# Eleven idle products of TensorE in the two gaps of a routing chain

## The chip, the cores and the metric

The kernel runs on one core of one Trainium2 chip. The metric is device time in microseconds, the median of several runs. A profiled execution gives the rows shown below; it is an execution of its own, with its own time.

## The reference

A graph layer, a linear attention and a mixture of experts on 1250 rows of 512 numbers. What matters here is the last part, the mixture:

```
x  = x + gnn(xn, ...) + mix(xn, ...)          # xn = layernorm(x)
xt = layernorm(x)
logits = xt @ Ws + bs                         # 1250 x 8
probs  = softmax(logits); prob_max = max(probs); routes = argmax(probs)
y[e]   = gelu(xt @ W1[e] + b1[e]) @ W2[e] + b2[e]
out    = x + prob_max * y[routes]
```

Each row goes through one of eight experts, the one with its largest logit.

## The kernel before

The rows stand in 10 tiles of 125 (t). The kernel is written by hand, one program for each engine, and the engines wait for each other by semaphores (`wait_ge`). TensorE takes its products in the order in which they are written. The names below are those of the code.

At the end of the graph layer TensorE turns the updated rows (`x2_turn`, line 817) and forms the logits (`route`, line 824), with products of 128 x 8. Then follows the routing chain:

- VectorE scales the logits, finds the largest of each row and writes the expert one-hot `oh16` (line 1407). ScalarE and VectorE form `prob_max`; it goes with the row's mean and deviation into `factors`, which SyncE's queue stores to `x1_rows` in DRAM (line 470).
- TensorE waits for `route_ok` 1 and multiplies the one-hot by triangles and ones (ten products of line 863, one of line 866). That counts the rows of each expert and gives each row its place.
- VectorE makes of this the row one-hot `row_hot` and `chunk_tag` (lines 1414 to 1435). The rows are put in 17 chunks of 128, each of one expert.
- TensorE waits for `route_ok` 2 and multiplies them (ten products of line 872). The result is the list of the rows of each chunk, which VectorE turns into `get_i` (line 1444) and `out_i`.
- TensorE then runs `MOE_UP` = 12 idle products (line 875): the identity by a constant of 250 columns, in float32, written to a part of bank 5 that nobody reads.
- GpSimd waits for the stores of all rows, for the store of `factors` (`fac_st`) and for `get_i` (`id_ok`), and then gathers the chunks by indirect DMA (line 507), eight of them ahead.

For each chunk c ScalarE normalizes the gathered rows (`xs_norm`, line 1745), TensorE turns them (`xs_turn`, line 883), ScalarE copies the result out of the bank (line 1752), and TensorE runs `up` (line 892, eight products with the weights of the chunk's expert), `h_turn` (line 902) and `down` (line 569, six products). The order on TensorE is xs_turn(0), up(0), xs_turn(1), and then h_turn(c), up(c+1), xs_turn(c+2), down(c). Meanwhile the rest of the second expert weight is split in a high and a low part, by ScalarE (`w2_high`, line 1702) and by VectorE (`w2_low`, line 1377, after `out_i`).

Of the kernel before, what the change touches and what calls it, by code (L numbers as in the profile page):

```python
# [34 lines left out]
WIN = 250  # L35
# [22 lines left out]
RESET_AT = 511  # L58
HALF = 112
MOE_UP = 12  # L60
LEFT = 25
RUN_UP = 10

# [48 lines left out]
def build(nc, x, edge_src, edge_dst, edge_w, consts, halves, biases, small, fold, wqkv, wp, bvt, w1f, w2f, b2f, out):  # L112
    with ExitStack() as ctx:
# [20 lines left out]
        def const(name):  # L134
            a, w = CONSTS[name]
            return cst[:, a:a + w]
# [13 lines left out]
        ident, ones = const("ident"), const("ones")  # L150
# [142 lines left out]
        bank = [banks[:, i, :] for i in range(8)]  # L293
# [232 lines left out]
        def _(pe):  # L526
# [7 lines left out]
            for i in range(NL):  # L534
                pe.wait_ge(hot_ok, next(n for n, m in enumerate(MARKED) if i < m) + 1)
                for h in range(2):
                    mm = pe.matmul(bank[1 + h][:, 0:NBH * LC], half("before")[0:TP, :],
                                   hot[:, i, h * NBH:(h + 1) * NBH, :].rearrange("p b c -> p (b c)"),
                                   start=(i == 0), stop=(i == NL - 1))
# [5 lines left out]
                      start=True, stop=True).then_inc(total_ps, 1)  # L545
# [65 lines left out]
            for k in range(2):  # L611
                mm = pe.matmul(bank[4][0:TP, 0:MD].rearrange("p (a n) -> p a n", a=2),
                               bm_col[:, k:k + 1].to_broadcast([128, TP]), w1g[:, :, k, :],
                               start=(k == 0), stop=(k == 1))
# [22 lines left out]
            for k in range(KD):  # L637
                pe.matmul(bank[5][0:TP, 256:256 + E], ones[:, 0:TP], little("ws")[:, k * E:(k + 1) * E], start=(k == 0),
                          stop=(k == KD - 1), skip_group_check=True)
# [57 lines left out]
            for n in range(PCOLS // 2):  # L697
                pe.wait_ge(sort_hot, n + 1)
                pe.wait_ge(sort_act, n + 1)
                for j in range(2):  # L700
                    for v in range(VT):
                        mm = pe.matmul(bank[1 - v // 2][:, v % 2 * NCH:(v % 2 + 1) * NCH], row_1h[:, n % RS, v, :, j],  # L702
                                       chunk_1h[:, n % RS, :, j], start=(n == 0 and j == 0 and v % 2 == 0),
                                       stop=(n == PCOLS // 2 - 1 and j == 1), skip_group_check=True)
# [126 lines left out]
            def both(step, w):  # L831
                step(2 * w)
                step(2 * w + 1)
# [23 lines left out]
            both(x2_turn, 4)  # L857
            both(route, 4)

            pe.wait_ge(route_ok, 1)  # L860
            for t in range(NT):
                n = NT - t
# [2 lines left out]
                               stop=False, skip_group_check=True)  # L865
            mm = pe.matmul(bank[7][0:TP, 0:NT * E], half("before")[0:TP, 0:TP], oh16[:, :, :].rearrange("p t e -> p (t e)"),
                           start=False, stop=True, skip_group_check=True)
            mm.then_inc(route_ps, 1)

            pe.wait_ge(route_ok, 2)  # L870
            for t in range(NT):
                mm = pe.matmul(bank[6][:, 0:NC], row_hot[:, t, :], chunk_tag[:, t, :], start=(t == 0), stop=(t == NT - 1))
            mm.then_inc(route_ps, 1)
            for _ in range(MOE_UP):
                pe.matmul(bank[5][:, 0:WIN], ident, const("cols"), start=True, stop=True)
# [56 lines left out]
        def _(dve):  # L932
# [66 lines left out]
            def pick(i):  # L999
# [7 lines left out]
                left = NB  # L1007
                while left > LEFT:
                    half_ = -(-left // 2)
# [3 lines left out]
                with nc.allow_low_precision(reason="whole numbers up to SLOTS, one of them not zero"):  # L1013
                    dve.tensor_reduce(slot_i[:, a:b], slot_p[:, 0:LEFT, 0:b - a].rearrange("p b c -> p c b"), X,
                                      ALU.max).then_inc(pick_ok, 1)
# [469 lines left out]
        def _(act):  # L1485
# [4 lines left out]
            def x_sums(a, b):  # L1490
                act.wait_ge(ld_x[next(i for i, (_, n) in enumerate(X_PARTS) if a < n)], 32)
                for t in range(a, b):
                    last = act.activation(q_sb[:, t, :], rec[:, t, 0:D], ACT.Copy, accum_out=x_sum[:, 0, t:t + 1])
                last.then_inc(sum_ok, b - a)
                act.wait_ge(sum_ok, b)
                act.activation(x_sum[:, 1, a:b], x_sum[:, 0, a:b], ACT.Copy, scale=-D ** -1.5).then_inc(mean_ok, b - a)
# [18 lines left out]
            def norm(t):  # L1515
                act.wait_ge(rstd_ok, next(g for g, (_, b) in enumerate(STATS) if t < b) + 1)
                if t >= 2:
                    act.wait_ge(xT_ps, t - 1)
                act.activation(xn[:, t % 2, :], rec[:, t, 0:D], ACT.Identity, bias=nmr[:, t:t + 1],
                               scale=rstd[:, t:t + 1]).then_inc(xn_ok, 1)  # L1520
# [339 lines left out]
```

## Time and profile before

| | |
|---|---|
| median of 3 runs | 494.15 us (493.7 to 494.18) |
| the profiled execution | 493.5 us |
| its span | 491.4 us |
| TensorE busy | 424.5 us (86%) |
| VectorE busy | 366.9 us (75%) |
| ScalarE busy | 298.3 us (61%) |
| GpSimd busy | 194.8 us (40%) |
| share of TensorE in the chain that ended last | 64% |

The span runs from the first to the last instruction of the program; the profiled execution's time has 2.1 us more. In the rows, PE is TensorE, DVE is VectorE, ACT is ScalarE, POOL is GpSimd and SP is SyncE; PEld is TensorE's weight load, and L863 is line 863 of the kernel. PEclk is the clock that TensorE was granted, as a share of full speed: 1.00 is 2.4 GHz and 0.50 is 1.2 GHz. Shares of busy time are means over stages with different limits.

### The profile page before, as it was taken

Reading aid. Unit: us, or ns where it says so; the run is one execution under the profiler, and the core shown is the slowest. Engines: PE = TensorE matmul, PEld = TensorE weight load, DVE = VectorE, ACT = ScalarE, POOL = GpSimd, SP = SyncE. Lnnn points to the kernel's source line nnn. Section 1 sums busy time; section 2 is a strip of 40 time slices with the busy share of each in tenths; the row PEclk is TensorE's granted clock in tenths of the full one; section 3 lists DMA queues with packets and bytes.
Section 4 is the critical chain, followed back from the end, with each engine's and each line's share of the span. In section 5 each row is a group of like instructions: output and inputs, shape, how many; then the busy total and the mean of one; then the engine's idle time right before and its main releaser. Section 6 shows DMA issues by size and latency. Waiting matters only on the chain.

```text
span 491.4 us, 8811 instructions
## 1 busy us (share of the span) xinstructions
PE 424.5 (86%) x2701; PEld 343.4 (70%) x2701; DVE 366.9 (75%) x717; ACT 298.3 (61%) x845; POOL 194.8 (40%) x160
## 2 busy tenths in 40 slices
PE   3665999999999999999777777899898957999992
PEld 1454887888887788877555555799876746788881
DVE  6786688877786888698999998478279874455552
ACT  4577999988897123363777777554335662666550
POOL 0378878688887787870000000000000008254321
PEclk9878999999999999999999999999999858999998
DMA  7992000000000000005000000000006964243210
GB/s 228 284 250 49 1 3 3 1 4 2 3 3 1 2 2 3 2 3 191 2 1 2 1 2 0 3 1 0 1 1 258 412 225 128 74 120 110 68 65 16
DMA packets 15742, 31.07 MB, mean 63 GB/s; under 512 B 7652, under 2 KB 8283, under 8 KB 14675
## 3 DMA queue, kind: packets, MB, share of 16 engines
q1 hardware_dynamic: 9266, 23.21, 14.6%
q0 software_dynamic: 6432, 7.31, 7.5%
q8 instruction: 24, 0.39, 0.3%
q14 instruction: 20, 0.16, 0.1%
HBM read 24.90 MB, written 7.37 MB: 66 GB/s over the span
## 4 chain that ended last, share of the span: by engine, by line
PE 64%; ACT 14%; DVE 10%; issue 6%; DMA 3%; POOL 1%; SPq 1%; ACTq 0%; DVEq 0%; POOLq 0%
PE banks L569 25%; PE banks L739 9%; PE banks L892 7%; PE banks L758 4%; ACT adj L1646 4%; PE banks L751 2%; ACT q_sb L1580 2%; PE banks L824 2%; PE banks L650 2%; PE banks L883 2%; ACT k_sb L1580 1%; DVE chunk_1h L1214 1%; DMA x_rows<-factors 1%; ACT q_sb L1563 1%; PE banks L731 1%
## 5 line engine op out<-in xcount | busy, mean ns | idle before, releaser
L496 POOL DMA_INDIRECT slots<-record,row_i x116 | 153.7, 1325 | 40.7 <-issue 40.7
L507 POOL DMA_INDIRECT rec<-x_rows,get_i x17 | 18.7, 1098 | 190.7 <-DMA x_rows<-factors 185.8
L1646 ACT ACTIVATE adj<-banks x108 | 58.4, 588 | 27.9 <-PE banks L739 26.8
L569 PE MATMUL banks<-w_hi,xT_hi 128*125 128x512 f32 (+1 forms) x160 | 61.5, 385 | 5.7 <-DVE xT_lo L1085 5.7
L739 PE MATMUL banks<-d_hot,s_hot 128*128 128x251 f16 x432 | 60.0, 276 | 0.2
L569 PE MATMUL banks<-w_lo,xT_hi 128*125 128x512 f32 (+1 forms) x160 | 60.1, 375 | 0.0
L569 PE MATMUL banks<-w_hi,xT_lo 128*125 128x512 f32 (+1 forms) x160 | 60.0, 375 | 0.0
L569 PEld LDWEIGHTS banks<-w_hi,xT_hi 128*125 128x125 f32 x160 | 30.9, 193 | 12.0 <-issue 6.1
L739 PEld LDWEIGHTS banks<-d_hot,s_hot 128*128 128x128 f16 x432 | 33.5, 98 | 7.5 <-issue 0.7
L569 PEld LDWEIGHTS banks<-w_lo,xT_hi 128*125 128x125 f32 x160 | 30.9, 193 | 5.8
L569 PEld LDWEIGHTS banks<-w_hi,xT_lo 128*125 128x125 f32 x160 | 30.6, 191 | 6.1
L516 POOL DMA_INDIRECT out<-o_sb,out_i x17 | 17.1, 1005 | 40.9 <-DVE o_sb L1462 40.9
L1268 DVE TENSOR_TENSOR d_hot<-col,keys 128x2000 f16<-128x2000 f16 (+1 forms) x28 | 32.3, 1153 | 0.0
L731 PE MATMUL banks<-hlf 128*128 128x1 f16 x108 | 18.3, 170 | 16.1 <-ACT adj L1646 16.1
L1276 DVE TENSOR_TENSOR s_hot<-s_one,parts 128x2048 f16<-128x2048 f16 x26 | 31.6, 1215 | 0.0
L1457 DVE TENSOR_TENSOR y_sb<-banks,b_sb 128x512 f32<-128x512 f32 x17 | 11.8, 691 | 26.2 <-PE banks L569 26.2
L731 PEld LDWEIGHTS banks<-hlf 128*128 128x128 f16 x108 | 10.4, 96 | 28.9 <-issue 26.9
L1580 ACT ACTIVATE q_sb<-q_sb,hmax 125x64 f32<-125x64 f32 x80 | 26.7, 335 | 4.3 <-DVE hmax L1113 4.2
L1609 ACT ACTIVATE row_1h<-row_one,sort_f 125x128 f16<-125x128 f16 x54 | 19.7, 432 | 13.8 <-DVE row_one L1208 8.0
L1580 ACT ACTIVATE k_sb<-k_sb,hmax 125x64 f32<-125x64 f32 x80 | 26.6, 333 | 0.0
L702 PE MATMUL banks<-chunk_1h,row_1h 125*128 125x216 f16 x216 | 22.8, 258 | 3.2 <-DVE chunk_1h L1214 2.2
L1617 ACT ACTIVATE xT_hi<-banks 128x500 fp32r<-128x500 f32 x10 | 5.9, 588 | 30.6 <-PE banks L663 30.6
(297 smaller groups left out, 1083.1 us busy)
## 6 DMA issues: line engine op xcount, KB each, us to landing
w_raw<-in_w2f SPq DMA_DIRECT2D x4, 1024.0 KB, 8.1
w_raw<-in_wqkv SPq DMA_DIRECT2D x3, 1024.0 KB, 15.2
x_rows<-rec SPq DMA_DIRECT2D x10, 224.0 KB
w1a<-in_w1f SPq DMA_DIRECT2D x1, 2048.0 KB, 7.8
w1b<-in_w1f SPq DMA_DIRECT2D x1, 2048.0 KB, 16.5
b_sb<-in_b2f SPq DMA_DIRECT2D x1, 2048.0 KB, 22.9
slots<-record,row_i POOLq DMA_INDIRECT x116, 2.6
rec<-in_x SPq DMA_DIRECT2D x1, 1120.0 KB
```

The source lines that it names most:

```text
L496: pool.indirect_dma_start(slots, bass.IndirectOffsetOnAxis(ap=row_i[:, c:c + 1], axis=0), record[:, c, :], None).then_inc(slot_st, 16)
L569: mm = pe.matmul(dst, ab, cd, start=(i == 0), stop=(i == n - 1))
L702: mm = pe.matmul(bank[1 - v // 2][:, v % 2 * NCH:(v % 2 + 1) * NCH], row_1h[:, n % RS, v, :, j], chunk_1h[:, n % RS, :, j], start=(n == 0 ...
L731: pe.matmul(flat_banks[:, bass.ds(at_new, 1)], before, zero_col, start=True, stop=False, skip_group_check=True)
L739: mm = pe.matmul(flat_banks[:, bass.ds(at_in, AW)], s_hot[:, n % DB, i, q, :, j], d_hot[:, n % DB, q, :, j], start=False, stop=(i == WT - ...
L758: mm = pe.matmul(hid_at(w), msg[:, t, GH:MD], adjw[:, t, w, 0:WIN], start=(t == 0), stop=(t == NT - 1), skip_group_check=True)
L892: mm = pe.matmul(bank[1][:, 0:F], xsT[:, c % 2, k, :], w1_sb[k // 2][:, k % 2, bass.ds(e * F, F)], start=(k == 0), stop=(k == KD - 1))
L1268: dve.tensor_tensor(d_hot[:, r, 0:k, 0:WIN, :], col_2[:, :, :].unsqueeze(1).to_broadcast([128, k, WIN, 2]), of_keys(1).to_broadcast([128, ...
L1276: last = dve.tensor_tensor(s_hot[:, r, :, :, :, :], s_one[:, n % 2, :, :, :].unsqueeze(1).to_broadcast(shape), both.unsqueeze(3).to_broadc ...
L1580: last = act.activation(ah, ah, ACT.Exp, bias=hmax[:, i, h:h + 1], accum_out=hsum[:, i, h:h + 1])
L1609: last = act.activation(row_1h[:, n % RS, VD, :, j], row_one[:, n % 2, :, j], ACT.Copy, scale=sort_f[:, 2 * n + j:2 * n + j + 1])
L1646: act.activation(adj[:, bass.ds(w, BW2)], flat_banks[0:TP, bass.ds(out_at, BW2)], ACT.Copy).then_inc(win_ok, 1)
```

## The change

Before TensorE waits for the expert one-hot it now runs four more idle products, and before it waits for the row one-hot seven more. They have the operands and the target of line 875, carry no semaphore and their result is read by nobody. The twelve of `MOE_UP` stay. Nothing else is changed.

```
+ROUTE_UP = (4, 7)
...
             both(route, 4)
 
+            for _ in range(ROUTE_UP[0]):
+                pe.matmul(bank[5][:, 0:WIN], ident, const("cols"), start=True, stop=True)
             pe.wait_ge(route_ok, 1)
             for t in range(NT):
                 n = NT - t
...
                            start=False, stop=True, skip_group_check=True)
             mm.then_inc(route_ps, 1)
 
+            for _ in range(ROUTE_UP[1]):
+                pe.matmul(bank[5][:, 0:WIN], ident, const("cols"), start=True, stop=True)
             pe.wait_ge(route_ok, 2)
             for t in range(NT):
                 mm = pe.matmul(bank[6][:, 0:NC], row_hot[:, t, :], chunk_tag[:, t, :], start=(t == 0), stop=(t == NT - 1))
```

## Rows read from the trace of the kernel before

**Rows 1.** The page: the span, and the granted clock of TensorE in 40 slices

```profile
span 491.4 us, 8811 instructions
...
PEclk9878999999999999999999999999999858999998
```

**Rows 2.** Chain that ended last, in order of time: start us, us, what

```profile
398.25 6.43 DMA x_rows<-factors
...
404.72 0.75 issue
405.47 4.23 DMA rec<-x_rows,get_i
...
410.75 0.65 PE banks L883 x4
...
412.86 3.53 PE banks L892 x8
...
418.40 1.99 PE banks L892 x8
...
422.44 1.81 PE banks L892 x8
...
476.31 1.80 PE banks L892 x8
```

**Rows 3.** Timeline of TensorE: start, us, line, tiles, count [idle before]

```profile
392.30 3.22 PE L824 MATMUL banks<-sml,x2T 128*125 128x8 f32 x16 [0.25 <-ACT x2T L1697]
...
397.73 1.23 PE L863 MATMUL banks<-oh,hlf 125*125 125x80 f16 x10 [2.21 <-DVE oh L1407]
...
398.82 0.31 PE L866 MATMUL banks<-oh,hlf 125*125 125x80 f16 x1
...
402.87 0.44 PE L872 MATMUL banks<-chunk_tag,row_hot 125*128 125x17 f16 x10 [3.75 <-DVE chunk_tag L1435]
...
403.16 6.86 PE L875 MATMUL banks<-cst 128*128 128x250 f32 x24
```

**Rows 4.** Timeline of VectorE, the same columns

```profile
397.44 0.24 DVE L1407 TENSOR_TENSOR oh<-cst,best 125x80 f16<-125x80 f32 x1
...
399.16 0.17 DVE L1414 TENSOR_SCALAR cnt_i<-banks 125x8 int32<-125x8 f32 x1 [0.94 <-PE banks L866]
...
402.48 0.34 DVE L1435 TENSOR_TENSOR chunk_tag<-chunk_hot,cst 125x170 f16<-125x170 f32 x1
...
403.64 0.18 DVE L1444 TENSOR_SCALAR get_i<-idf 128x17 int32<-128x17 f32 x1
```

**Rows 5.** Line 875, records at the lower and at the higher clock

```profile
L875 PE MATMUL banks<-cst x6: 622/624/627, 403.7 to 405.8; 128*128 128x250 f32 x6
...
L875 PE MATMUL banks<-cst x10: 374/375/375, 407.7 to 409.6; 128*128 128x250 f32 x10
```

**Rows 6.** Stretches: us, busy (count) by engine, PEclk, DMA share, GB/s

```profile
core 0: us, PE busy (x) PEld busy (x) DVE busy (x) ACT busy (x) POOL busy (x), PEclk, DMA share, GB/s
28.65:34.20 5.55, 5.55 (x13) 4.38 (x14) 5.18 (x5) 4.83 (x9) 4.64 (x4) 0.50 1.08 209
48.05:51.30 3.25, 3.25 (x10) 2.56 (x9) 0.94 (x2) 3.25 (x15) 2.64 (x3) 0.50 0.09 2
51.40:54.70 3.30, 3.30 (x16) 2.64 (x15) 1.38 (x2) 3.18 (x13) 2.69 (x3) 1.00 0.08 2
392.70:395.30 2.60, 2.60 (x14) 2.60 (x13) 1.92 (x7) 1.50 (x3) 0.00 (x0) 0.50 0.86 306
403.15:406.30 3.15, 3.15 (x14) 2.59 (x12) 3.08 (x7) 1.04 (x2) 0.83 (x1) 0.50 0.00 0
406.35:409.70 3.35, 3.35 (x18) 2.97 (x16) 3.35 (x2) 0.00 (x0) 2.74 (x3) 1.00 0.29 79
409.75:413.10 3.35, 1.14 (x7) 0.67 (x6) 0.74 (x1) 2.11 (x3) 2.74 (x3) 1.00 0.54 154
413.20:416.50 3.30, 3.30 (x10) 2.53 (x9) 0.00 (x0) 0.00 (x0) 2.51 (x3) 0.50 0.66 181
```

More of the change, by code:

```diff
@@ L60 @@
 MOE_UP = 12
+ROUTE_UP = (4, 7)
 LEFT = 25
@@ L858, in _ @@
             both(route, 4)
+            for _ in range(ROUTE_UP[0]):
+                pe.matmul(bank[5][:, 0:WIN], ident, const("cols"), start=True, stop=True)
             pe.wait_ge(route_ok, 1)
@@ L868, in _ @@
             mm.then_inc(route_ps, 1)
+            for _ in range(ROUTE_UP[1]):
+                pe.matmul(bank[5][:, 0:WIN], ident, const("cols"), start=True, stop=True)
             pe.wait_ge(route_ok, 2)
```

## The prediction

> **What bounds the kernel now.** I read the page first. It gives the span of 491.4 us and the clock strip of TensorE (PE): nine tenths or more nearly everywhere after the start, but 8, 5 and 8 tenths in slices 32 to 34, which are the 37 us from 381 to 418 us [rows 1]. The routing chain lies there. Second, I read the chain that ended last, in order of time. The reader is to see that from 398.25 us it leaves PE: it runs through the store of the factors, which lands 6.43 us later at 404.69 us, then 0.75 us of issue on GpSimd (POOL), then the first gather with 4.23 us to its landing, and comes back to PE only at 410.75 us, with the turn of the first gathered chunk. From there it is mostly PE work, chunk after chunk, to the last up at 476.31 us: up(0), eight products, takes 3.53 us; up(1) 1.99 us; up(2), and later ones like it, 1.8 us [rows 2]. So from 398.25 to 410.75 us PE is not on the path, and what PE does there costs nothing as long as it is in time.
>
> Third, I read PE's own list for that stretch. The last logit products (L824) start at 392.30 and end at 395.52 us. The expert one-hot products (L863, L866) start at 397.73 us after 2.21 us of idling and end at 399.13 us. The row one-hot products (L872) start at 402.87 us after 3.75 us of idling. The twelve idle products that the kernel already has (L875) follow from 403.16 to 410.02 us [rows 3]. These two idle times are the two gaps of the change. Fourth, the other engines' rows at the same times: VectorE (DVE) writes the expert one-hot until 397.68 us; its row steps start at 399.16 us and end with chunk_tag at 402.82 us; get_i, which POOL needs for the gather, is done at 403.82 us [rows 4]. POOL waits for the store of the factors and for get_i, and the store came last, at 404.69 us. The slack of the routing chain is 404.69 - 403.82 = 0.87 us. It is the most important number here.
>
> **What one idle product costs.** The kernel's own L875 products are of the same form as the added ones: twelve of them have 24 records, so two records each. At the lower clock six records start over 2.1 us, 0.42 us apart; at the higher ten start over 1.9 us, 0.21 us apart [rows 5]. A product is 0.84 us at 1.2 GHz and 0.42 us at 2.4 GHz. The stretches say which clock holds: it is at 0.50 from 392.70 to 395.30 us, although PE is busy all of that time (with products of 8 columns), and at 0.50 until 406.30 us, 1.00 after [rows 6]. So the clock is already down when the first gap begins.
>
> **First edit, four products ahead of the expert one-hot.** They can start at about 395.35 us, a little before the last logit product ends, as L875 starts at 403.16 us under the tail of L872 [rows 3]. Eight records at 0.42 us end at 395.35 + 3.34 = 398.69 us. The one-hot products would have started at 397.73 us, so they start 0.96 us late. Their own length is 1.40 us at the lower clock [rows 3]; if that holds, they end at 400.09 us. All that hangs on them moves by the same 0.96 us: the row steps of DVE, chunk_tag (from 402.82 to 403.78 us) and get_i (from 403.82 to 404.78 us) [rows 4]. The slack takes 0.87 us of that and 0.09 us reaches POOL. If the clock rises while they run, the bound on the other side is four products at 0.42 us = 1.7 us inside the 2.21 us gap: nothing late. I take +0.09 us, since the rows show the clock down. Behind the late one-hot on DVE are also the remaining three w_lo pieces of the second expert weight; down(0) is the first to need them, and it comes after up(1), past 420 us, so their move is hidden.
>
> The Trainium skill (TensorE: Matmul & The Clock Gate, the table on why this matters for kernels) advises that no long idle gap stay between bursts of products, or the clock falls back. By that rule filling the gaps holds the clock, the four products take 1.7 us and nothing is late. The trace differs in this place: the clock was down before the gap, under busy small products [rows 6], so here it would have to be raised first, and the sum by the rows is +0.09 us and not 0.
>
> **Second edit, seven products ahead of the row one-hot.** They start where the expert products end, 400.09 us, and must be through by 403.78 us, when chunk_tag is there: 3.69 us. Fourteen records take 2.94 us at the higher clock, which fits, and 5.88 us at the lower, which is 2.19 us too long. With x records at the lower clock, 0.42x + 0.21(14 - x) = 3.69 gives x = 3.6: the seven are hidden if the clock rises by about 401.6 us. When it rises I bound by other rises in this trace. After L875 began it took 403.16 to at least 406.30 us, about 3.2 us; in the stretch from 48.05 us it also took some 3.3 us; from 28.65 us it was still down after 5.55 us of full work [rows 6]. Counted from the first added product at 395.35 us, these give 398.5 to at least 400.9 us, and the seven are hidden. That counts the 1.40 us of small one-hot products in the middle as work, and the stretch at 392.70 us shows that small products do not raise the clock by themselves [rows 6]. That is the weak step. Counted anew from 400.09 us, 3.16 us gives 403.25 us: 7.5 records at the lower clock and 6.5 at the higher end at 404.62 us, 0.84 us late. I take the first count, because 3.34 us of the kind that raised the clock before stand unbroken in front of the small ones.
>
> **What the clock gives back.** L863 and L866 take 1.40 us and L872 takes 0.44 us [rows 3]; both at the higher clock could shorten the chain, but by less than it is late and inside the slack, so nothing of it reaches the end. The existing L875 would run at the higher clock from its start at about 404.05 us: 24 records, 5.04 us, ending at 409.1 us instead of 410.02 us. Nothing waits for that, since PE then waits for the gathered chunk at 410.75 us [rows 2]. And the stage that pays for a low clock on the path, up(0) with 3.53 us, comes after this wait: the clock is 1.00 from 409.75 to 413.10 us while PE is busy for only 1.14 us of 3.35 us, and 0.50 from 413.20 to 416.50 us [rows 6]. The change adds no work there; it makes the quiet time ahead of it about 0.9 us longer. So up(0) stays slow and the expected gain does not arrive.
>
> **The sum.** +0.09 us (first edit) + 0 (second) - 0 (clock, off the path) = about +0.1 us. The profiled execution was 493.5 us (span 491.4 us and 2.1 us around it), which gives 493.6 us. The median of the runs is 494.15 us, 0.65 us above the profiled one, so against the median the forecast is 494.3 us. A measurement tells 0.2% of this kernel, 1.0 us, from no change.
>
> **Rivals.** *The clock stays low in the seven products.* If the small one-hot products break the count, the second overrun is 0.84 us with a rise at 403.25 us and 5.88 - 3.69 = 2.19 us without one. POOL is then later by 0.93 to 2.28 us in all, and with it the gather, the first turn and everything after: 495.1 to 496.4 us. It decides, as a loss of over 1.0 us, when the clock rises later than about 403.4 us. For it: a rise that was still not there after 5.55 us of full work, and busy small products that raised nothing [rows 6]. Against it: the two rises of 3.2 and 3.3 us. Part of the loss can come back, since the twelve products of L875 would then end later and nearer to up(0), 1.5 us cheaper with the clock up. Chance 0.30 for the part over 1.0 us.
>
> *up(0) at the higher clock.* If the clock falls later or not at all before up(0), its eight products take about 1.9 instead of 3.53 us, as up(1) and up(2) do [rows 2]: -1.6 us, 492.6 us, faster than before. It decides if the clock holds until some 414.5 us, past most of up(0). Against it: the quiet stretch that preceded the fall gets longer, not shorter. For it: the moments of rise and fall sit at no instruction of the program, and the change moves the work in front of them. Chance 0.14.
>
> The Trainium skill (TensorE: Matmul & The Clock Gate, Part 1) says that the point of the rise varies from run to run of one kernel. By it both rivals would occur in some executions and not in others, before and after alike; the trace of one execution cannot show that.
>
> The rest, 0.56, is the forecast: 0 to 1.0 us more than before, 494.1 to 495.1 us, with the expert one-hot some 1 us late and the slack absorbing it. The faster case (0.14) is below the range and the end of the slow case is its top; the low end leaves the forecast the scatter of the runs: 493.3 to 496.4 us. Chances: faster 0.14, within 0.2% 0.56, slower 0.30.
>
> **What the profile after would show.** L863 starts near 398.7 us with no idle time before it, and not 397.7 us. The clock goes to 1.00 between 398.5 and 401.6 us. L872 starts at about 403.8 us, after a wait for chunk_tag (right) or straight behind the idle products (the slow rival). The first gather starts within 0.2 us of 405.47 us. L875 ends near 409 us, and up(0) still takes 3 us or more. The forecast is wrong if POOL's first gather waits for get_i by 1 us or more, or if up(0) takes 2 us.

## The result

The changed kernel is slower. Its median is 496.15 us over 17 runs (492.29 to 497.89), against 493.64 us over 17 runs of the kernel before (491.59 to 496.54); the ratio is 1.0049 with a 95% interval from 1.0028 to 1.0070. That is about +2.4 us. The forecast was 494.3 us, with 0.56 on no difference and 0.30 on slower; the time lies inside the range, near its top, and the case that came about is the first rival. The range stood on 494.15 us for the kernel before, from 3 runs; its 17 runs beside the changed kernel gave 493.64 us, and from there the same sum would have ended at 493.64 + 2.28 = 495.9 us, below the measured 496.15 us.

The profiled execution of the changed kernel has a span of 495.2 us, 3.8 us more than before. The page, its span and the granted clock in 40 slices:

```profile
span 495.2 us, 8855 instructions
...
PEclk9877999999999999999999999999999658999998
```

Slices 32 to 34 read 9, 6 and 5 tenths where before they read 8, 5 and 8 [rows 1]: more of the stretch is at the lower clock. Then the chain that ended last, in order of time (start us, us, what), to be laid beside [rows 2]:

```profile
397.46 3.54 PE banks L862 x8
400.99 0.97 PE banks L866 x10
...
402.13 5.08 PE banks L874 x14
...
407.96 0.74 issue
408.70 5.02 DMA rec<-x_rows,get_i
...
414.76 0.65 PE banks L888 x4
...
416.95 3.38 PE banks L897 x8
```

Before, the chain left TensorE (PE) at 398.25 us and ran through the store of the factors. Now it runs through PE the whole way: the four added products (L862), the expert one-hot (L866, L869), the seven added products (L874), the row one-hot (L877), get_i on VectorE (DVE), and only then the gather. The added work is on the path. PE's own list shows it (start us, us, engine, line, tiles, count, [idle before]), beside [rows 3]:

```profile
393.93 3.52 PE L825 MATMUL banks<-sml,x2T 128*125 128x8 f32 x16
397.31 3.68 PE L862 MATMUL banks<-cst 128*128 128x250 f32 x8
400.79 1.17 PE L866 MATMUL banks<-oh,hlf 125*125 125x80 f16 x10
401.82 0.31 PE L869 MATMUL banks<-oh,hlf 125*125 125x80 f16 x1
401.93 5.28 PE L874 MATMUL banks<-cst 128*128 128x250 f32 x14
407.04 0.40 PE L877 MATMUL banks<-chunk_tag,row_hot 125*128 125x17 f16 x10
407.30 5.31 PE L880 MATMUL banks<-cst 128*128 128x250 f32 x24
```

There is no idle time left in front of L866 and L877: neither waits for its input any more, both wait for idle products. The inputs' own times, on DVE, beside [rows 4]:

```profile
399.37 0.24 DVE L1412 TENSOR_TENSOR oh<-cst,best 125x80 f16<-125x80 f32 x1
...
405.47 0.34 DVE L1440 TENSOR_TENSOR chunk_tag<-chunk_hot,cst 125x170 f16<-125x170 f32 x1
...
407.69 0.18 DVE L1449 TENSOR_SCALAR get_i<-idf 128x17 int32<-128x17 f32 x1
...
407.86 6.69 DVE L1382 TENSOR_TENSOR w_lo<-w_raw,w_hi 128x2048 fp32r<-128x2048 f32 x3
```

The expert one-hot was ready at 399.37 + 0.24 = 399.61 us and used at 400.79 us, 1.18 us later, where before the step took 0.05 us (397.68 to 397.73 us): 1.13 us late. chunk_tag was ready at 405.81 us and used at 407.04 us: 1.23 us, 1.18 us more than before. Stretches give the clock (us; busy time and count of PE, PEld, DVE, ACT, POOL; PEclk; DMA share; GB/s), beside [rows 6]:

```profile
389.10:391.90 2.80, 2.80 (x15) 2.80 (x16) 1.84 (x4) 2.04 (x2) 0.00 (x0) 0.50 1.07 436
...
397.30:400.70 3.40, 3.40 (x9) 2.73 (x10) 2.34 (x13) 1.75 (x2) 0.00 (x0) 0.50 0.99 347
...
401.95:405.95 4.00, 4.00 (x12) 3.29 (x12) 3.44 (x15) 3.97 (x4) 0.00 (x0) 0.50 0.11 2
406.50:412.60 6.10, 6.10 (x38) 5.10 (x36) 5.11 (x7) 0.00 (x0) 3.60 (x2) 1.00 0.14 33
...
416.60:419.50 2.90, 2.55 (x6) 2.11 (x7) 0.00 (x0) 0.13 (x1) 1.99 (x4) 0.50 0.61 187
```

The clock is at 1.2 GHz in the first three stretches, from 389.1 us through the logit products and the four to most of the seven. It is still there until 405.95 us and back at 2.4 GHz by 406.50 us, over 8 us after the first idle product and some 4 us after the start of the seven. In the last stretch, that of up(0), it is at 1.2 GHz again.

GpSimd (POOL), its first gathers:

```profile
408.70 2.32 POOL L508 DMA_INDIRECT rec<-x_rows,get_i  x1 [189.31 <-DVE out_i L1450]
411.33 1.86 POOL L508 DMA_INDIRECT rec<-x_rows,get_i  x1 [0.30 <-issue]
...
415.67 0.95 POOL L508 DMA_INDIRECT rec<-x_rows,get_i  x1 [0.30 <-issue]
```

and, before, its first gather and what VectorE did meanwhile, from the lists of both engines:

```profile
405.47 1.49 POOL L507 DMA_INDIRECT rec<-x_rows,get_i  x1 [185.82 <-DMA x_rows<-factors]
...
403.80 6.68 DVE L1377 TENSOR_TENSOR w_lo<-w_raw,w_hi 128x2048 fp32r<-128x2048 f32 x3
```

**Where the 3.8 us of span went.** I take the end of the last logit products as the mark ahead of the change: 395.52 us before, 393.93 + 3.52 = 397.45 us now. So 1.93 us are older than the change; the clock fell earlier in this execution, at about 389 us instead of 392.6 us, and slowed the logit products. From the mark to the first turn (L883 before, L888 now) it was 15.23 us and is 414.76 - 397.45 = 17.31 us: +2.08 us. That closes in three parts. get_i was done 8.30 us after the mark and is done 407.87 - 397.45 = 10.42 us after it: +2.12 us. From get_i to the gather's start it was 1.65 us, since POOL then waited for the factors, and is 0.83 us: -0.82 us. From the gather's start to the turn it was 5.28 us and is 6.06 us: +0.78 us, and the gather's own issue on POOL is 0.83 us longer, 2.32 us in place of 1.49. Sum: +2.08 us. up(0) is 3.38 instead of 3.53 us, and all that follows the first turn is 0.2 us shorter.

The second and the third part belong together. The first w_lo piece of VectorE starts right behind get_i, and the first gather's issue ended 405.47 + 1.49 - 403.82 = 3.14 us after get_i before and ends 408.70 + 2.32 - 407.87 = 3.15 us after it now, though it started 1.65 us after get_i then and 0.83 us after it now. So the 0.87 us by which get_i was ahead of the store bought nothing even in the execution from which it was read: an issue that started earlier would only have taken longer. From get_i to the first turn it was 6.93 us and is 6.89 us. All of get_i's delay reaches the turn.

### The profile page after: what moved, and what is told of

It is laid out like the page before. It is cut to its first block, busy times and chain, and to the rows that moved or that the text cites. A ratio compares the mean times of both kernels' runs of the same rounds, so it can differ in the third digit from the quotient of the medians.

```text
span 495.2 us, 8855 instructions
## 1 busy us (share of the span) xinstructions
PE 433.2 (87%) x2723; PEld 351.1 (71%) x2723; DVE 366.9 (74%) x717; ACT 298.7 (60%) x845; POOL 195.7 (40%) x160
## 4 chain that ended last, share of the span: by engine, by line
PE 66%; ACT 13%; DVE 9%; issue 6%; DMA 2%; POOL 1%; SPq 1%; ACTq 0%; DVEq 0%; POOLq 0%
PE banks L570 25%; PE banks L740 9%; PE banks L897 7%; PE banks L759 4%; ACT adj L1651 4%; PE banks L752 2%; ACT q_sb L1585 2%; PE banks L825 2%; PE banks L651 2%; PE banks L888 2%; ACT k_sb L1585 1%; DVE chunk_1h L1219 1%; ACT q_sb L1568 1%; PE banks L732 1%; PE banks L874 1%
## 5 line engine op out<-in xcount | busy, mean ns | idle before, releaser
L703 PEld LDWEIGHTS banks<-chunk_1h,row_1h 125*128 125x128 f16 x216 | 19.9, 97 | 6.3 <-DVE chunk_1h L1219 4.7
```

## The experiments

Each ratio is to runs of the kernel before on the same chip, in turn with it; the times of different chips are not compared. The first four ran on one chip (seven only with 7 runs and double with 4, the others with 12), the other eight on another. For the profiles I give the same two numbers everywhere: the time from the end of the last logit products to the first turn, and the length of up(0). Before they are 15.23 and 3.53 us, in the changed kernel 17.31 and 3.38 us.

**Four products only.**

```
-ROUTE_UP = (4, 7)
+ROUTE_UP = (4, 0)
```

> Only the four products ahead of the expert one-hot; the seven are left out. Theory (the added products run at the lower clock, overrun their gap, and make get_i the last thing that GpSimd waits for): the expert one-hot starts 1.0 to 1.1 us late, the slack of 0.87 us takes most, so +0.1 to +0.6 us against the kernel before. Rival (the loss has nothing to do with the overrun, but with the quiet time and the clock ahead of up(0), or with the chance position of the clock's changes): no overrun visible, or the whole loss of about 2.4 us is here already.

Measured: 1.0013 (0.9988 to 1.0037), no difference that can be told. PE in its profile:

```profile
394.77 3.59 PE L862 MATMUL banks<-cst 128*128 128x250 f32 x8
398.20 0.69 PE L866 MATMUL banks<-oh,hlf 125*125 125x80 f16 x10
398.75 0.23 PE L869 MATMUL banks<-oh,hlf 125*125 125x80 f16 x1
...
410.80 0.60 PE L888 MATMUL banks<-cst,xs 128*128 128x128 f32 x4
```

The four products start at 394.77 us and the one-hot products at 398.20 us, while the one-hot was ready at 397.07 us: 1.13 us after it, 1.08 us more than before, and in the change it is 1.13 us more. But the clock was up again when they ran, L866 and L869 took 0.78 us instead of 1.40, and a good part of the delay came back. The distance to the first turn is 410.80 - 394.92 = 15.88 us, 0.65 us more than before, and up(0) takes 1.99 us. The overrun is as the theory had it. Its slack did nothing here either: POOL waited for get_i, and its first gather was issued in 2.33 us. The time by itself tells +0.6 us neither from zero nor from 1.8 us.

**Seven products only.**

```
-ROUTE_UP = (4, 7)
+ROUTE_UP = (0, 7)
```

> Only the seven products ahead of the row one-hot. Theory: the clock is down when they begin, 14 records at 0.42 us are 5.9 us in a gap of 3.7 us; the row one-hot starts up to 2.2 us late, of which the slack takes 0.87 us: +0.5 to +1.9 us. Rival: same time as before within 0.5 us, the row one-hot waits for chunk_tag as before.

Measured: 1.0083 (1.0051 to 1.0115), about +4 us and more than was expected. The theory gave the overrun alone; what it lacked follows with the table below.

```profile
398.78 1.23 PE L866 MATMUL banks<-oh,hlf 125*125 125x80 f16 x10 [2.21 <-DVE oh L1412]
...
399.98 5.90 PE L874 MATMUL banks<-cst 128*128 128x250 f32 x14
405.72 0.40 PE L877 MATMUL banks<-chunk_tag,row_hot 125*128 125x17 f16 x10
...
413.40 0.63 PE L888 MATMUL banks<-cst,xs 128*128 128x128 f32 x4 [2.12 <-ACT xs L1750]
```

The seven take 5.7 us of a gap in which chunk_tag was ready at 403.87 us; the row one-hot starts at 405.72 us, 1.85 us late. The distance to the first turn is 413.40 - 396.57 = 16.83 us and up(0) takes 3.61 us. So the seven alone are enough for a loss at least as large as that of the change. They have 2.9 us of work at the higher clock and 5.9 us at the lower, and the clock was at half from 388.5 us to 405.3 us, nearly the end of the seven.

**The same products, shorter.**

```
+SHORT = 100
...
             for _ in range(ROUTE_UP[0]):
-                pe.matmul(bank[5][:, 0:WIN], ident, const("cols"), start=True, stop=True)
+                pe.matmul(bank[5][:, 0:SHORT], ident, const("cols")[:, 0:SHORT], start=True, stop=True)
```

and the same for the seven.

> Four and seven products as in the change, but of 100 columns in place of 250, so that at the lower clock four take 1.3 us and seven 2.3 us and both fit their gaps (2.2 and 3.7 us). Theory (the overrun is the cost): nothing is late, the time is that of the kernel before within 0.5 us. Rival (adding work there costs in another way: clock, instruction stream, the quiet time ahead of up(0)): about +2.4 us as in the change.

Measured: 1.0005 (0.9976 to 1.0035).

```profile
396.94 2.01 PE L863 MATMUL banks<-cst 128*128 128x100 f32 x8
399.30 1.23 PE L867 MATMUL banks<-oh,hlf 125*125 125x80 f16 x10 [0.35 <-DVE oh L1413]
...
400.50 3.29 PE L875 MATMUL banks<-cst 128*128 128x100 f32 x14
404.43 0.43 PE L878 MATMUL banks<-chunk_tag,row_hot 125*128 125x17 f16 x10 [0.65 <-DVE chunk_tag L1441]
404.72 7.67 PE L881 MATMUL banks<-cst 128*128 128x250 f32 x24
412.25 0.63 PE L889 MATMUL banks<-cst,xs 128*128 128x128 f32 x4
```

Both waits are back, 0.35 and 0.65 us of idle time ahead of the one-hot products, and the loss is gone. The distance is 412.25 - 397.08 = 15.17 us, and up(0) takes 1.99 us. Eleven more products cost nothing that can be told by being there (the interval allows 1.7 us); what costs is that they don't fit their gaps, and what they do to the clock behind them, which follows below. The clock did not rise while they ran either; it was at half through them and through the first 4.5 us of the twelve existing products (stretches, columns as above):

```profile
396.90:404.40 7.50, 6.54 (x34) 6.04 (x34) 5.66 (x28) 5.79 (x5) 0.00 (x0) 0.50 0.56 162
404.80:409.20 4.40, 4.40 (x14) 3.61 (x12) 4.33 (x7) 0.96 (x2) 2.69 (x2) 0.50 0.01 4
```

**Twice the change.**

```
-ROUTE_UP = (4, 7)
+ROUTE_UP = (8, 14)
```

> Eight and fourteen products, twice the change. Theory: the clock rises while they run, but both gaps are overrun; expert one-hot late by 3.8 to 4.5 us, row one-hot by a further 2 us or more: +4.5 to +7 us against the kernel before. Rival: the same +2.4 us as the change.

Measured: 1.0109 (1.0059 to 1.0160), about +5.4 us, from 4 runs; the distance is 417.76 - 397.40 = 20.36 us, +5.1 us. Inside the range of the theory.

**Hold back w_lo.** The gather's issue of 2.32 us was not foreseen. In the profile after, the three gathers under DVE's w_lo pieces are issued in 1.86 to 2.32 us and the five after them in 0.94 to 0.96 us. In the kernel before:

```
+            dve.wait_ge(ld_rec[0], 16)
-            for i in range(1, 4):
-                w2_low(i)
+            w2_low(1)
+            w2_low(2)
             dve.wait_ge(exp_of, 1)
             dve.wait_ge(ld_b2, 16)
             h_copy(0)
+            w2_low(3)
```

> The kernel before, with the three remaining w_lo pieces of VectorE held back until the first gather has landed, and the last of them after h_copy(0). Theory (a w_lo piece of VectorE that runs holds up GpSimd's issue of a gather to its own end): the first gather's issue takes 0.95 us and not 1.49 to 2.33 us, and the first turn comes 0.5 to 1.4 us earlier; -0.5 to -1.4 us in all. Rival (the issue is long for another reason, such as being the first of its queue): no change in its 1.5 to 2.3 us, and 0 us in all.

Measured: 0.9973 (0.9939 to 1.0007), unclear. POOL's list and DVE's:

```profile
408.56 1.01 POOL L507 DMA_INDIRECT rec<-x_rows,get_i  x1 [188.69 <-DVE out_i L1445]
...
412.39 2.94 POOL L507 DMA_INDIRECT rec<-x_rows,get_i  x1 [0.30 <-issue]
```

```profile
412.22 4.49 DVE L1377 TENSOR_TENSOR w_lo<-w_raw,w_hi 128x2048 fp32r<-128x2048 f32 x2 [4.42 <-DMA rec<-x_rows,get_i]
```

The first three gathers are issued in 0.95 to 1.01 us each, with DVE idle, and the fourth, beside a w_lo piece, takes 2.94 us. The mechanism is shown: a w_lo piece that runs holds the gather's issue. The Trainium skill (SBUF — State Buffer, "SBUF: two separate sides") says that VectorE and GpSimd share one pair of ports as an exclusive lock, held for a whole instruction, and that a VectorE instruction with two inputs in SBUF, as w_lo's subtraction is, contends only with a GpSimd instruction that reads SBUF. The trace agrees in so far as the issue took 1.01 us without a w_lo piece and 2.3 to 2.9 us beside one; the gather's indices, get_i, lie in SBUF, but that it is their reading that is held is not shown. The time is unclear, and PE's list says why the gain is small:

```profile
407.06 7.54 PE L875 MATMUL banks<-cst 128*128 128x250 f32 x24
414.44 0.60 PE L883 MATMUL banks<-cst,xs 128*128 128x128 f32 x4
```

The twelve idle products run 7.54 us here, mostly at the lower clock, and end only when the first turn starts: the turn waits for them and no longer for the gather. The normalized chunk was ready on ScalarE at 413.11 us, 1.33 us ahead of the turn. The distance is 15.01 us.

**Idle products ahead of up(0).** In the kernel before:

```
             xs_turn(0)
+            for _ in range(3):
+                pe.matmul(bank[5][:, 0:WIN], ident, const("cols"), start=True, stop=True)
             e = up(0)
```

> The kernel before, with three idle products of 250 columns between xs_turn(0) and up(0), in the 1.5 us in which TensorE waits for ScalarE's copy. Theory (up(0) is slow because the clock falls in the quiet time just ahead of it): up(0) takes 2.0 us where it took 3.5 us; -0.3 to -1.5 us, since in some executions it is at the higher clock already. Rival (three products are not enough, or they overrun at the lower clock by 1.0 us): 0 to +1 us.

Measured: 0.9945 (0.9911 to 0.9980), more than up(0) can give. So it was run again:

> The kernel before with three idle products ahead of up(0), once more, since its gain of 0.55% was more than the 1.6 us that up(0) can give. Theory: -0.3 to -1.6 us. Rival (the first measurement was chance): 0 within 0.5 us.

Measured: 0.9991 (0.9961 to 1.0022). The two together leave a gain of some tenths of a per cent possible and not shown. In both profiles up(0) takes 2.0 us, but so it does in that of w_lo held back, without the three products, so these profiles don't show that they did anything.

**Both edits.**

> Both edits together on the kernel before: w_lo pieces held back, three idle products ahead of up(0). If both theories hold and the gains add: -0.8 to -2.5 us, first gather issued in 0.95 us and up(0) at 2.0 us. If neither, 0 to +1 us.

Measured: 0.9969 (0.9935 to 1.0003), unclear; distance 413.41 - 398.86 = 14.55 us, up(0) 1.99 us.

**The changed kernel with more idle products behind it** (`MOE_UP` at 16, and three ahead of up(0)).

> The changed kernel with MOE_UP at 16 in place of 12 and three idle products between xs_turn(0) and up(0). Theory (in the changed kernel the twelve products run at the higher clock, end 2 us before the gathered chunk is there, and up(0) then falls to the lower clock, which is a second part of the loss beside the overrun): up(0) takes 2.0 us in place of 3.4 us, and the kernel loses 1.4 us of its distance to the kernel before. Rival (the overrun alone is the loss): the time of the changed kernel, +2.4 us, or more.

Measured: 1.0051 (1.0021 to 1.0080), with up(0) at 1.99 us and the distance at 17.26 us. The changed kernel was then measured on the same chip too:

> The changed kernel once more, as the measure for the next one on the same chip. Both theories: +2 to +3 us against the kernel before.

> The changed kernel with MOE_UP at 16 and three idle products ahead of up(0), now beside the changed kernel itself. Its first profile showed up(0) at 1.99 us, yet its time was no nearer to the kernel before. Theory (a slow up(0) is a part of the loss): 1 to 1.5 us less than the changed kernel in the comparison against before. Rival (what is won at up(0) is lost again in the longer run of idle products where these run at the lower clock; the overrun of the gaps is the whole loss): the same as the changed kernel within 0.5 us.

Measured: the changed kernel 1.0040 (1.0008 to 1.0073), the other 1.0008 (0.9979 to 1.0037), with up(0) at 3.78 and 1.99 us. That is 1.6 us less, as the theory had it, but the first measurement was 1.0051. The means of the two measurements of each, 1.0045 and 1.0030, are 0.7 us apart, less than their intervals. That up(0) is repaired is shown by both profiles, by the two edits together and not by either alone; by the times alone, how much of the loss it is stays open.

The second profile of the changed kernel also shows how much hangs on the moment of the rise:

```profile
398.93 3.30 PE L862 MATMUL banks<-cst 128*128 128x250 f32 x8
402.07 0.70 PE L866 MATMUL banks<-oh,hlf 125*125 125x80 f16 x10
...
402.69 3.20 PE L874 MATMUL banks<-cst 128*128 128x250 f32 x14
406.60 0.41 PE L877 MATMUL banks<-chunk_tag,row_hot 125*128 125x17 f16 x10 [0.72 <-DVE chunk_tag L1440]
...
414.42 0.63 PE L888 MATMUL banks<-cst,xs 128*128 128x128 f32 x4 [2.25 <-ACT xs L1750]
```

Here the clock rose under the four products (at half until 401.50 us, full from 401.80), the seven take 3.20 us and the row one-hot waits 0.72 us for chunk_tag, as the forecast had it. The distance is 414.42 - 399.07 = 15.35 us, nearly that of before; the twelve products ended 2.25 us ahead of the turn, and up(0) is slow.

Four executions with these eleven products were profiled, two of the changed kernel and two with more products behind. The clock rose 8.8 and 8.5 us after the first added product in the first profile of each, and 2.8 and 4.8 us after it in the second, with the same instructions up to there. The second profile with more products is the forecast's own case, since its small one-hot products still ran at the lower clock (1.34 us) and the seven were hidden:

```profile
406.32 0.41 PE L877 MATMUL banks<-chunk_tag,row_hot 125*128 125x17 f16 x10 [0.67 <-DVE chunk_tag L1442]
...
414.14 0.63 PE L888 MATMUL banks<-cst,xs 128*128 128x128 f32 x4 [0.56 <-ACT xs L1752]
```

Its distance is 414.14 - 397.90 = 16.24 us, 1.01 us more than before, where the forecast had 0.09 us: the first overrun passed to the turn nearly whole.

**w_lo held back, three products ahead of up(0), and eight instead of twelve** (`MOE_UP = 8`), from the kernel before.

> The kernel before with w_lo pieces held back, three idle products ahead of up(0), and MOE_UP at 8 in place of 12. Theory (with twelve products at the lower clock TensorE comes late to the first turn and hides what the earlier gather gains; eight take 6.7 us at most and are out of the way): the first turn no longer waits behind idle products, -1 to -2.5 us. Rival (with eight the clock is not up in time for the first chunk, and up(0) takes 3.5 us): 0 to +1 us.

Measured: 0.9947 (0.9912 to 0.9981), about 2.6 us faster than the kernel before, and faster than the changed kernel, whose interval on that chip lies above 1. It was measured once, and the gain of the three products alone did not repeat, so its size is uncertain.

```profile
407.00 6.06 PE L875 MATMUL banks<-cst 128*128 128x250 f32 x16
413.03 0.64 PE L883 MATMUL banks<-cst,xs 128*128 128x128 f32 x4
```

The distance is 413.03 - 399.36 = 13.67 us, the shortest of all, and up(0) takes 1.99 us. The eight products end just as the turn starts; the chunk was ready on ScalarE at 412.88 us, so they hardly held it up.

**The profiles side by side.** Distance from the last logit products to the first turn, length of up(0), their sum, and the ratio to the kernel before:

| kernel | distance | up(0) | sum | ratio |
|---|---|---|---|---|
| before | 15.23 | 3.53 | 18.76 | 1 |
| short | 15.17 | 1.99 | 17.16 | 1.0005 |
| four only | 15.88 | 1.99 | 17.87 | 1.0013 |
| changed kernel, both profiles | 17.31, 15.35 | 3.38, 3.78 | 20.69, 19.13 | 1.0049, 1.0040 |
| seven only | 16.83 | 3.61 | 20.44 | 1.0083 |
| double | 20.36 | 3.58 | 23.94 | 1.0109 |
| changed kernel with more products | 17.26, 16.24 | 1.99, 1.99 | 19.25, 18.23 | 1.0051, 1.0008 |
| w_lo held back | 15.01 | 2.00 | 17.01 | 0.9973 |
| three ahead of up(0) | 15.37, 15.30 | 1.99, 1.99 | 17.36, 17.29 | 0.9945, 0.9991 |
| both | 14.55 | 1.99 | 16.54 | 0.9969 |
| both, eight products | 13.67 | 1.99 | 15.66 | 0.9947 |

For the kernels with added products the sums follow the ratios, once the shortened products stand for the kernel before: their times are equal (1.0005), while its one profile has a slow up(0). For those with changes of 0.3% and less one profile says little, as the two ratios of the three products ahead of up(0) show. Against 17.16 us the changed kernel's mean of 19.91 us is +2.75 us, where +2.4 us were measured; seven alone +3.3 us, where about 4 were measured; four alone +0.7 us, where 0.6 were; the changed kernel with more products +1.6 us, where 1.5 were; double +6.8 us, where 5.4 were, with an interval from 2.9 to 7.9. By its two profiles, 1.16 us of the changed kernel's 2.75 is distance and 1.59 us is up(0). This split rests on the one profile that stands for the kernel before; against that kernel's own profile the 2.75 us would be 1.15 us.

## Why the prediction was right, and where it was wrong

The range held; the likeliest case, no difference, did not, and the measured loss of 2.4 us is over ten times the +0.1 us of the sum. That the time lies in the range is in part luck: the top of the range was the slow rival's 2.28 us on a median of 3 runs that was 0.5 us above that of 17, and a slow up(0), which the sum had at nothing, makes up a part of the loss. By its steps:

- *The price of a product and the first overrun* were right: 0.96 us late was forecast, 1.13 us measured in the profile after and 1.08 us in that of the four alone.
- *The second edit, taken as hidden,* is the step that failed first: "I take the first count". In the profile after, the rise came over 8 us after the first added product and some 4 us after the start of the seven, and they overran by 1.18 us, between the 0.84 and 2.19 us of the rival. Of the four profiles with these eleven products two show this case and two that of the forecast. It is a matter of the execution, and the bounds "about 3.2 us" and "over 5.55 us" from the trace of before were a fair warning: 0.30 on the rival was low for what came in two of four. That the seven are the costly half is borne out by the two halves run alone, 1.0083 against 1.0013.
- *The slack of 0.87 us*, "the most important number here", failed too, in every profile with a late get_i. It came from one profile, in which the store of the factors landed late. In five of the six profiles of kernels with nothing added or nothing late ahead of get_i (the shortened products, w_lo held back, three products ahead of up(0) twice, and eight products) POOL was released by DVE's list and not by the store; in the one with both edits it was the store. And where the store was late, as before, the slack was no slack, for the next reason.
- *The w_lo pieces, "so their move is hidden",* and nothing in the sum for the gather itself: they start right behind get_i and hold the gather's issue. A gather that starts right behind get_i meets the first w_lo piece at its beginning, one that waits for the factors meets its end, and for both the issue ends 3.14 to 3.15 us after get_i. The term for the first edit was therefore its whole overrun, about +1.0 us, and not +0.09 us: 1.01 us was measured where the clock did as forecast.
- *up(0) stays slow* was right for the profile: 3.38 to 3.78 us in all four with seven or fourteen products of full size and no more filling behind them. As a term of the sum it was wrong. In the profiles of the other nine experiments up(0) takes 2.0 us. In those without the seven at full length, the twelve existing products run mostly at the lower clock, take 7.1 to 8.0 us, last nearly to the first turn and leave up(0) at the higher clock. With the clock raised earlier they take 5.31 us, end 2.0 to 2.3 us ahead of the turn, and the clock falls in the quiet time or as up(0) begins. The change does bring the clock up sooner, and by the profiles that costs some 1.6 us at up(0). That the kernel before is mostly like the former is argued from profiles of its near relatives and their equal times; it has one profile of its own, and that one has a slow up(0). How often up(0) is slow in either kernel is not shown.
- *Its own signs of being wrong:* up(0) did not take 2 us. POOL does wait for get_i now and no longer for the store, but no row shows when the store landed, so whether it waited the 1 us stays open. The first gather starts 11.25 us after the last logit products instead of 9.95 us, 1.30 us late where at most 0.2 us was forecast.
- *The shift to the median* was small beside the scatter of 5 us between runs, which may come in part from the moment at which the clock falls ahead of the change, 1.93 us between the two profiles.

## What to carry to other kernels

Price idle products that are to raise the clock at the lower clock, where they take twice as long, and let them fit the gap at that price; here 100 columns fitted and 250 did not. Ask what existing idle products do once the clock is up sooner: here they ended earlier and left a quiet time ahead of work on the path. Filling that time, right ahead of up(0), had up(0) at 1.99 us in the changed kernel; from the kernel before, a gain by it alone was not shown. Before spending a slack, measure it in several profiles, and follow what else starts with the late result: here VectorE's next instructions moved with get_i and held the gather that the slack was counted for.

## What the runs showed of the hardware

- TensorE's clock came back 2.8 us after the first idle product in one execution of the changed kernel (398.93 us, full from 401.80 at the latest) and over 8 us after it in the other, with the same instructions; in two executions with more products behind them it was 8.5 and 4.8 us.
- Eleven products of 100 columns with short waits between them did not raise it; the clock was at half in their whole stretch.
- An indirect gather is issued in 0.95 to 1.01 us with VectorE idle, and in 1.49 to 2.94 us beside a float32 subtraction of 128 x 2048 on VectorE, which itself takes about 2.3 us. The first gather's issue ended 3.14 to 3.15 us after get_i, whether it started 0.83 or 1.65 us after it.
